# Attention and a gated FFN on one core: fp16 parts of queries and keys, and softmax steps taken in pairs

## The chip, the cores and the metric

The kernel runs on one core of a Trainium2 chip. The metric is the device time of one execution in microseconds, the median of several runs. The core has TensorE (matmuls, PE in the profile), VectorE (DVE), ScalarE (ACT), GpSimd (POOL) and SyncE (SP), which issues all the DMAs here. Each engine works its own instructions in the order in which they were written and waits for the others through semaphores.

## The reference

x has 2 batches of 1024 rows of 512 numbers, all fp32. Weights: Wq, Wk, Wv, Wo of 512 x 512; W1, W3 of 2048 x 512; W2 of 512 x 2048.

```python
xn = layernorm(x)
q, k, v = xn @ Wq.T, xn @ Wk.T, xn @ Wv.T          # 16 heads of 32
scores = q @ k.T / sqrt(32), causal                 # 1024 x 1024 per head
s = softmax(scores) @ v, heads joined, @ Wo.T
h = silu(xn @ W1.T) * (xn @ W3.T)                   # 2048 wide
g = silu(fwht(h) @ W2.T)                            # Walsh-Hadamard, normalised
out = x + s * g
```

## The kernel before, in words

Products that need fp32 accuracy are taken as three products of a high and a low part of each factor (hi x hi, hi x lo, lo x hi). The FFN, V and the probabilities use scaled fp16 parts; Q, K and everything that makes them use float32r parts.

Each of the two batches goes through three stages.

**project(b).** x is normalised (VectorE), transposed in 8 tiles (TensorE, `transpose_xn`, L1418) and split (`xt`, `x16`). TensorE then forms 16 groups of 12 matmuls for Q and K (`group`, L1453; four PSUM banks in turn) and 8 for V. ScalarE copies the high part of each group (L805), VectorE subtracts the low part (L1183), and SP stores both into `qk_parts` in DRAM. In batch 0 ScalarE first splits the weights (L776) as their DMAs land: three tiles of Wq, x, the fourth tile; then after group 1 the four tiles of Wk. VectorE subtracts in the same order, and normalises the second half of x after group 2.

**heads(b).** 16 heads of 12 steps each. `load_stack` brings for each head a stack of 96 rows, Q parts (hi, hi, lo) and K parts (hi, lo, hi), so that one matmul of 96 rows forms the three products. Two more rows hold the negated row maximum (hi and lo) against ones, so that the scores come out of TensorE with their maximum subtracted. The maxima of head n+1 are formed while head n runs: 8 query tiles in the order `MAX_ORDER`, in two matmuls of up to 512 columns for the four longer ones and one for the others (`maxima`, L1554), reduced by VectorE (L1249, or L1251 where it also masks) at the steps `MAX_AT`: 9, 10, 11 of the head before and 0, 1, 3, 4, 5. In batch 0, heads 1 to 15, six of the eight tiles are masked by a further small matmul (L1557) instead. At step 7 TensorE transposes the eight columns of maxima (`transpose_maxima`, L1563), after waiting for the last reduction; ScalarE and VectorE split them (L940, L1257) and two DMAs (L546) write them into the stack's rows for the next head's scores.

A step is a block of 128 keys by up to 512 queries (widths 512, 384, 256, 128, then 512 four times, then 512, 384, 256, 128). Of each step: TensorE forms the scores (`scores`, L1573; two steps are issued together at each even step, each into a bank of its own, and a step of 128 columns is formed 256 wide); ScalarE takes the exponential (`exp`, L868) into one of four buffers `expd`; POOL zeroes the masked triangle of the diagonal steps (`mask`, L699); ScalarE copies to fp16 (`probs_hi`, L878); VectorE subtracts the low part (`probs_lo`, L1264). In ScalarE's order the exponential of step g stands ahead of the copy of step g-1. TensorE multiplies with V in blocks of four steps (`context`, L1591, L1593) at steps 7, 10 and 15, that is step 3 of the next head.

Between these TensorE works off the FFN's 48 matmuls per head (`ffn`, L1613; `FFN_SHARE` says how many at each step). Its results go through ScalarE (`tanh`, L894, one at steps 1 and 7) and VectorE (`gate`, `hide`, L1286 and L1292). The next head's W1 and W3 tiles are scaled (L860) and copied (L931) by ScalarE at steps 1 to 3, and POOL subtracts their low parts in four pieces (`w13_low`, L707). ScalarE copies the output accumulator (`copy_o`, L884) at steps 4 and 8, and POOL joins its halves (`combine`, L713, L718).

In each step the order of an engine's work is written out by hand in its `heads`:

```python
for jm, r in MAX_PLAN.get(g - 1, []):     # VectorE: reductions of the step before
    maxima(n0 + jm, r)
if 1 <= g <= SLOTS:
    probs_lo(n0 * NS + g - 1)
```

**tail(b).** The context is transposed and multiplied with Wo (L1693, L1698); in batch 0 W2 goes through the rest of its Hadamard transform (L1678), its rows loaded by SP once all low parts are done; then the FFN's down projection (L1409 to L1411).

Of the kernel before, what the change touches and what calls it, by code (L numbers as in the profile page):

```python
# [29 lines left out]
P = 128  # L30
# [13 lines left out]
X_TOP = 2048.0  # L44
H_BACK = 2.0 ** -45
# [13 lines left out]
NS = len(STEPS)  # L59
MAX_ORDER = [7, 0, 5, 1, 6, 2, 4, 3]  # L60
NE = 4
# [35 lines left out]
SPLIT_WK_AFTER, ROOT_AFTER = 1, 2  # L97
BUSY_FIRST, BUSY_LAST = 42, 6
# [19 lines left out]

def build(nc, x, wq, wk, wv, wo, w1w3, w2, hadamard, out):

    qk_parts = nc.dram_tensor("qk_parts", [4, D, S], F32R, kind="Internal").ap()
# [4 lines left out]
    with ctx:  # L126
# [27 lines left out]
        g_scale = sb("g_scale", [P, JT], F32)  # L154
        w2_power, w2_scale, h_top, h_top_back, g_back = (
# [15 lines left out]
        with ExitStack() as r:  # L171
            qk_st = [sb(f"qk_st{i}", [P, 2, S], F32R, r) for i in (1, 2)]
# [4 lines left out]
        with ExitStack() as r:  # L177
# [4 lines left out]
            p_hi = [sb(f"p_hi{s}", [P, widths[s]], F16, r) for s in range(NS)]  # L182
            p_lo = [sb(f"p_lo{s}", [P, widths[s]], F16, r) for s in range(NS)]
            squares = sb("squares", [P, 2 * D], F16, r)
            sb("room_after_p", [P, 4 * KT * S - 2 * sum(widths) - 2 * D], F16, r)
# [3 lines left out]
            m_hi = sb("m_hi", [NT, P], F32R, r)  # L189
            m_lo = sb("m_lo", [NT, P], F32R, r)  # L190
            ones_r = sb("ones_r", [P, P], F32R, r)
            qk_lo3 = sb("qk_lo3", [P, W], F32R, r)
# [6 lines left out]
            with ExitStack() as q:  # L199
                qk_hi = [sb(f"qk_hi{i}", [P, W], F32R, q) for i in range(NB)]  # L200
                qk_lo = [*(sb(f"qk_lo{i}", [P, W], F32R, q) for i in range(NB - 1)), qk_lo3]
# [3 lines left out]
            expd = [*stage, sb("expd3", [P, W], F32, r)]  # L205
            scan = sb("scan", [P, 2, D], F32, r)
            sb("room_before_o", [P, 5 * P], F32, r)
            o_sb = [sb(f"o_sb{i}", [P, TPC, VN], F32, r) for i in range(NC)]
            rden = [sb(f"rden{i}", [P, TPC], F32, r) for i in range(NC)]
            qk_st.insert(0, sb("qk_st0", [P, 2, S], F32R, r))  # L210
# [11 lines left out]
        sb("room_after_g_lo1", [P, JT // 2 * D - P], F16)  # L222
# [9 lines left out]
        SB = [bank("s0"), bank("s1")]  # L232
# [16 lines left out]
        proj_ps, proj_hi_done, proj_lo_done = (sem(n) for n in ("proj_ps", "proj_hi_done", "proj_lo_done"))  # L249
        wv_in, wv_abs, bound_ps, v_scale_step, unscale_ps, unscale_done = (  # L250
# [43 lines left out]

        NQ = 2 * KT
# [102 lines left out]

        def diagonal(s):
# [1373 lines left out]
```

## Time and profile before

| | |
|---|---|
| median of 3 runs | 944.87 us (943.33 to 947.14) |
| the profiled execution | 944.66 us, its span 943.0 us |
| TensorE (PE) busy | 928.3 us, 98% |
| VectorE (DVE) busy | 728.0 us, 77% |
| ScalarE (ACT) busy | 625.5 us, 66% |
| GpSimd (POOL) busy | 339.0 us, 36% |
| granted TensorE clock | 0.999 of full speed |
| DMA | 110 MB |
| heads of batch 0 | 88 to 367 us of the span |
| heads of batch 1 | 556 to 829 us |

Matmuls overlap in the profile: the busy time of a matmul is longer than the distance to the next one's start, so that distance is what it costs.

### The profile page before, as it was taken

To read this page: it belongs to the slowest core of one execution; us is meant where nothing else is said; L and a number is where in the kernel's file an instruction comes from. 1 tells how busy PE (TensorE), PEld (TensorE's weight loads), DVE (VectorE), ACT (ScalarE), POOL (GpSimd) and SP (SyncE) were. 2 spreads that over 40 slices of the span, in tenths; PEclk is the share of its full clock that TensorE was granted. 3 is DMA by queue.
4 is the path that set the end of the run, shared out by engine and by line. 5 is a ranking of instruction groups with operands and counts; after the bars stand their busy time and mean duration, and the time that the engine had idled before them with its cause. 6 is when DMAs were issued, how large, how long until landed. Compare 5 with 4: busy or idle time off the path is not lost. (4 is left out here: it accounts for less than half of the span.)

```text
span 943.0 us, 19017 instructions
## 1 busy us (share of the span) xinstructions
PE 928.3 (98%) x6500; PEld 566.6 (60%) x6500; DVE 728.0 (77%) x1416; ACT 625.5 (66%) x1340; POOL 339.0 (36%) x591
## 2 busy tenths in 40 slices
PE   8999999999999999999999999999999999999997
PEld 7764566666666656744468656566665666575443
DVE  7886998998998988846665579989898899833343
ACT  4456889989889877833344358787887888833221
POOL 1896664665665442000000114344344353410000
PEclk9999999999999999999999999999999999999999
DMA  9797245544343414661236622323323232150111
GB/s 291 270 252 228 80 114 151 143 118 118 86 121 90 118 31 124 221 226 44 67 103 244 201 57 80 91 58 95 76 75 92 61 81 58 46 202 22 45 45 45
DMA packets 57920, 110.09 MB, mean 117 GB/s; under 512 B 5600, under 2 KB 22624, under 8 KB 57312
## 3 DMA queue, kind: packets, MB, share of 16 engines
q1 hardware_dynamic: 57824, 108.88, 38.9%
q8 instruction: 52, 0.85, 0.4%
q14 instruction: 44, 0.36, 0.1%
HBM read 79.23 MB, written 29.36 MB: 115 GB/s over the span
## 5 line engine op out<-in xcount | busy, mean ns | idle before, releaser
L1264 DVE TENSOR_TENSOR p_lo<-stages,p_hi 128x512 f16<-128x512 f32 (+2 forms) x288 | 201.7, 710 | 25.3 <-ACT p_hi L878 23.7
L1613 PE MATMUL f<-x_hi,w_lo 128*128 128x512 f16 x512 | 195.6, 382 | 0.0
L1613 PE MATMUL f<-x_lo,w_hi 128*128 128x512 f16 x512 | 194.8, 380 | 0.0
L1613 PE MATMUL f<-x_hi,w_hi 128*128 128x512 f16 x512 | 194.5, 380 | 0.0
L868 ACT ACTIVATE stages<-s 128x512 f32<-128x512 f32 (+2 forms) x288 | 150.6, 524 | 57.9 <-PE s L1573 55.5
L878 ACT ACTIVATE p_hi<-stages 128x512 f16<-128x512 f32 (+2 forms) x288 | 160.5, 557 | 25.6 <-POOL stages L699 16.4
L1573 PE MATMUL s<-qk_st 98*128 98x512 f32 (+2 forms) x384 | 129.9, 416 | 1.7 <-DMA qk_st<-m_lo 1.5
L699 POOL TENSOR_SCALAR_AFFINE_SELECT stages<-stages 128x128 f32<-128x128 f32 x192 | 61.4, 325 | 167.9 <-ACT stages L868 167.4
L707 POOL TENSOR_TENSOR w_lo<-w,w_hi 128x256 f16<-128x256 f32 x128 | 95.5, 775 | 55.2 <-ACT w_hi L931 52.8
L1251 DVE CUSTOM_DVE_ANT_0 m<-m,causal 128x1024 f32<-128x1024 f32 (+1 forms) x98 | 104.5, 1066 | 3.8 <-PE m L1554 2.7
L986 ACT ACTIVATE h_hi<-hidden 128x1024 f16<-128x1024 f32 x32 | 33.8, 1057 | 97.1 <-PE f L1411 97.1
L1332 DVE TENSOR_TENSOR h_lo<-hidden,h_hi 128x1024 f16<-128x1024 f32 x32 | 39.2, 1224 | 76.4 <-ACT h_hi L986 76.4
L1409 PE MATMUL f<-g_hi,h_hi 128*128 128x512 f16 x256 | 97.0, 379 | 0.0
L1410 PE MATMUL f<-g_lo,h_hi 128*128 128x512 f16 x256 | 97.0, 379 | 0.0
L1411 PE MATMUL f<-g_hi,h_lo 128*128 128x512 f16 x256 | 97.0, 379 | 0.0
L1554 PE MATMUL m<-qk_st 96*128 96x512 f32 (+3 forms) x256 | 92.7, 443 | 0.0
L1573 PEld LDWEIGHTS s<-qk_st 98*128 98x128 f32 x384 | 72.4, 191 | 15.3 <-DMA qk_st<-m_lo 3.2
L1613 PEld LDWEIGHTS f<-x_hi,w_lo 128*128 128x128 f16 x512 | 50.0, 98 | 52.1 <-issue 15.2
L1613 PEld LDWEIGHTS f<-x_lo,w_hi 128*128 128x128 f16 x512 | 50.3, 98 | 51.2 <-issue 13.5
L1591 PE MATMUL o<-vparts,p_hi 128*128 128x65 f16 x1152 | 78.0, 191 | 1.0 <-DVE p_lo L1264 1.0
L1591 PEld LDWEIGHTS o<-vparts,p_hi 128*128 128x128 f16 x1152 | 70.4, 96 | 11.0 <-issue 2.8
L1593 PE MATMUL o<-vparts,p_lo 128*128 128x33 f16 x1152 | 76.5, 178 | 0.0
(224 smaller groups left out, 1907.9 us busy)
## 6 DMA issues: line engine op xcount, KB each, us to landing
qk_st<-qk_parts SPq DMA_DIRECT2D x96, 256.0 KB, 4.3
w<-w1w SPq DMA_DIRECT2D x32, 512.0 KB, 3.6
qk_parts<-qk_hi SPq DMA_DIRECT2D x32, 256.0 KB, 3.5
qk_parts<-qk_lo SPq DMA_DIRECT2D x32, 256.0 KB, 4.4
scan<-w1w SPq DMA_DIRECT2D x12, 512.0 KB, 5.6
wht_in<-w SPq DMA_DIRECT2D x4, 1024.0 KB, 10.6
w_butterflied<-wht_in SPq DMA_DIRECT2D x4, 1024.0 KB, 5.7
x_in<-x SPq DMA_DIRECT2D x16, 256.0 KB, 2.9
```

The lines of the kernel that those rows point to most:

```text
L707: pool.tensor_tensor(w13_lo[n % 2][at], w13[at], w13_hi[n % 2][at], ALU.subtract).then_inc(w13_lo_done, 1)
L868: act.activation(expd[q % NE][:, 0:end - need], SB[q % 2][:, 0, need - start:end - start], ACT.Exp).then_inc(exp_done, 1)
L878: act.activation(p_hi[s][:], expd[q % NE][:, 0:end - need], ACT.Copy).then_inc(p_hi_done, 1)
L1251: dve.tensor_tensor_reduce(out=bank, in0=bank, in1=causal[:, S - width:S], scale=1.0, scalar=LOWEST, op0=ALU.add, op1=ALU.max, accum_out=m ...
L1264: dve.tensor_tensor(p_lo[s][:], expd[q % NE][:, 0:end - need], p_hi[s][:], ALU.subtract).then_inc(p_lo_done, 1)
L1409: pe.matmul(o, a_hi, b_hi, start=first, stop=False)
L1410: pe.matmul(o, a_hi, b_lo, start=False, stop=False)
L1411: return pe.matmul(o, a_lo, b_hi, start=False, stop=last)
L1554: mm = pe.matmul(bank[:, at:end], q[0:STACK, t * P:(t + 1) * P], k[0:STACK, at:end], start=True, stop=True)
L1573: pe.matmul(SB[q % 2][:, 0, 0:end - start], k_st[n % NH % 3][0:STACK + 2, k * P:(k + 1) * P], q_st[n % NH % 3][0:STACK + 2, start:end], st ...
L1591: pe.matmul(O[:, 0, first:first + VN], p_hi[s][:, at:at + P], v, start=k == 0 and t == c * TPC, stop=False, skip_group_check=True)
L1613: mm = pe.matmul(F[m][:, 0, :], w, v, start=k == 0, stop=k == GMM - 1)
```

## The change: what it does, and the diff

Queries, keys and the rows of maxima are kept as fp16 parts instead of float32r. So that fp16 holds them, Q and K each get a power of two as a scale, found in batch 0 from the sum of squares of Wq and Wk (eight Squares on ScalarE, two small matmuls, nine small operations of VectorE); the exponential takes the factor back as a per-partition scale. The first score and maxima widths are no longer padded to 256. The two steps (2u, 2u+1) become one pair u: their scores lie side by side, across the border of two PSUM banks, and exponential, mask, copy and subtraction are one instruction per pair. `expd` has two buffers of 1024 columns, no longer in `stages`, and SP no longer waits for the last low part before it loads rows of W2. Cut to its core:

```diff
-NE = 4
+NE = 2
+NP = NS // 2
+SUM_OF_WK_AFTER = 5
-    qk_parts = nc.dram_tensor("qk_parts", [4, D, S], F32R, kind="Internal").ap()
+    qk_parts = nc.dram_tensor("qk_parts", [4, D, S], F16, kind="Internal").ap()
-            m_hi = sb("m_hi", [NT, P], F32R, r)
+            m_hi = sb("m_hi", [NT, 2 * P], F16, r)[:, 0:P]
+            expd = [sb(f"expd{i}", [P, 2 * W], F32, r) for i in range(NE)]
-        SB = [bank("s0"), bank("s1")]
+        S_PAIR = bank("s", 2)
+        SB = [S_PAIR[:, i:i + 1, :] for i in range(2)]
         def score_cols(c, k):
-            return min(need, end - 2 * P), need, end
+            return need, need, end
+        def pair_bank(u):
+            w1, w0 = pair_widths(u)
+            return S_PAIR[:].rearrange("p b w -> p (b w)")[:, W - w1:W + w0]
 # SP
             def load_weight(b, i):
                 if i >= 5:
                     sp.wait_ge(split_lo, split_no(b, i) - 4)
+                    if b == 0:
+                        sp.wait_ge(wqk_sum, i - 4)
-                sp.wait_ge(p_lo_done, (n0 + NH) * NS)
                 if b == 0:
                     sp.wait_ge(wht_stored, D // P * 16)
+                    sp.wait_ge(w13_sum, SCAN_FIRST)
 # POOL
-            def mask(q):
-                pool.wait_ge(exp_done, q + 1)
-                e = expd[q % NE][:, 0:P]
-                pool.affine_select(out=e, in_=e, compare_op=ALU.is_ge, fill=0.0, base=0, pattern=[[1, P]],
+            def mask(n, u):
+                pool.wait_ge(exp_done, n * NP + u + 1)
+                e = expd[(n * NP + u) % NE][:, 0:2 * pair_widths(u)[0]].rearrange("p (a c) -> p a c", a=2)[:, :, 0:P]
+                pool.affine_select(out=e, in_=e, compare_op=ALU.is_ge, fill=0.0, base=0, pattern=[[0, 2], [1, P]],
                                    channel_multiplier=-1).then_inc(mask_done, 1)
-                            pool.wait_ge(exp_done, n * NS + 4 + piece)
+                            pool.wait_ge(exp_done, n * NP + 2 + piece // 2)
                             w13_low(n + 1, piece)
 # ScalarE
+            def wqk_squares(i):
+                act.wait_ge(ssq_ready, 3)
+                if i:
+                    act.wait_ge(wqk_sum, i)
+                act.activation(qk_squares[:], raw[i % 5], ACT.Square, accum_out=qk_ssq[:, i:i + 1]).then_inc(wqk_sum, 1)
             def qk(g):
-                    act.activation(qk_hi[g % NB][:], group_bank(g), ACT.Copy,
-                                   scale=SCALE if QK_GROUPS[g][1] == 0 else 1.0).then_inc(proj_hi_done, 1)
+                    m = QK_GROUPS[g][1]
+                    act.wait_ge(qk_scale_step, qk_scale_steps(m))
+                    act.activation(qk_hi[g % NB][:], group_bank(g), ACT.Copy, scale=qk_scale[:, m:m + 1]
+                                   ).then_inc(proj_hi_done, 1)
                     split_weight(b, KT - 1)
+                    for i in range(KT):
+                        wqk_squares(i)
                     if g == SPLIT_WK_AFTER:
                         for i in range(KT, 2 * KT):
                             split_weight(b, i)
+                            if b == 0:
+                                wqk_squares(i)
             def exp(q):
+                u = q % NP
                 act.wait_ge(scores_ps, q + 1)
                 after(act, p_lo_done, q - NE + 1)
+                act.activation(expd[q % NE][:, 0:sum(pair_widths(u))], pair_bank(u), ACT.Exp,
+                               scale=qk_back[:, 0:1]).then_inc(exp_done, 1)
             def probs_hi(q):
+                if masked_pair(u):
+                    act.wait_ge(mask_done, masks_upto(n, u))
+                act.activation(p_hi[u][:], expd[q % NE][:, 0:sum(pair_widths(u))], ACT.Copy
             def heads(b):
-                    if g < SLOTS:
-                        exp(n0 * NS + g)
-                    if 1 <= g <= SLOTS:
-                        probs_hi(n0 * NS + g - 1)
+                    if g < SLOTS and g % 2 == 0:
+                        exp(n0 * NP + g // 2)
+                    if g < SLOTS and g % 2 == 1:
+                        probs_hi(n0 * NP + g // 2)
 # VectorE
+            def scale_of_qk(m):
+                dve.wait_ge(wqk_sum_ps, m + 1)
+                dve.tensor_reduce(qk_power[:, at], wqk_sum_bank(m), axis=AX.X, op=ALU.add).then_inc(qk_scale_step, 1)
 ...
+                    if b == 0 and g == KT - 1:
+                        scale_of_qk(1)
             def heads(b):
-                    if 1 <= g <= SLOTS:
-                        probs_lo(n0 * NS + g - 1)
+                    if g < SLOTS and g % 2 == 1:
+                        probs_lo(n0 * NP + g // 2)
 # TensorE
                     group(g)
+                    if b == 0 and g == SUM_OF_WK_AFTER:
+                        sum_of_wqk(1)
-                bank, parts = max_parts(t) if t else (X[:, 0, 0:2 * P], [(0, 2 * P)])
+                bank, parts = max_parts(t)
             def scores(q):
-                if s == 0:
+                n, u = divmod(q, NP)
+                if u == 0:
                     pe.wait_ge(m_in, (n + 1) * 32)
-                after(pe, exp_done, q - 1)
+                after(pe, exp_done, q)
+                for s in (2 * u + 1, 2 * u):
+                    c, k = STEPS[s]
+                    start, _, end = score_cols(c, k)
+                    bank = SB[0][:, 0, W - (end - start):W] if s % 2 else SB[1][:, 0, 0:end - start]
+                    mm = pe.matmul(bank, k_st[n % NH % 3][0:STACK + 2, k * P:(k + 1) * P],
+                                   q_st[n % NH % 3][0:STACK + 2, start:end], start=True, stop=True)
+                mm.then_inc(scores_ps, 1)
```

## Rows read from the trace of the kernel before

**Rows 1.** Stretches of the heads; busy us (count) PE, PEld, DVE, ACT, POOL; clock, DMA.
```profile
88.30:366.60 278.30, 277.64 (x2405) 167.56 (x2405) 251.42 (x496) 242.33 (x556) 153.54 (x274) 1.00 0.40 106
545.00:829.00 284.00, 282.50 (x2355) 170.85 (x2353) 252.62 (x562) 228.38 (x530) 119.76 (x250) 1.00 0.27 70
```

**Rows 2.** Timeline, TensorE and VectorE: start us, us, what [idle <- releaser]; two heads.
```profile
238.80 0.68 DVE L1249 TENSOR_REDUCE mx<-xs 128x1 f32<-128x512 f32 x1
239.97 0.27 PE L1563 MATMUL xs<-ident,mx 128*8 128x128 f32 x1
...
676.54 0.57 PE L1573 MATMUL s<-qk_st 98*128 98x512 f32 x2
686.33 0.69 DVE L1251 CUSTOM_DVE_ANT_0 xs<-xs,causal 128x512 f32<-128x512 f32 x1
687.26 0.27 PE L1563 MATMUL xs<-ident,mx 128*8 128x128 f32 x1
...
693.60 0.57 PE L1573 MATMUL s<-qk_st 98*128 98x512 f32 x2
```

**Rows 3.** Timeline of TensorE, part of a head of batch 0.
```profile
241.72 0.38 PE L1613 MATMUL f<-x_hi,w_lo 128*128 128x512 f16 x1
241.94 0.38 PE L1613 MATMUL f<-x_hi,w_hi 128*128 128x512 f16 x1
241.97 0.81 PE L1554 MATMUL m<-qk_st 96*128 96x512 f32 x2
242.63 0.39 PE L1613 MATMUL f<-x_lo,w_hi 128*128 128x512 f16 x1
242.67 0.58 PE L1573 MATMUL s<-qk_st 98*128 98x256 f32 x2
243.09 0.39 PE L1613 MATMUL f<-x_hi,w_lo 128*128 128x512 f16 x1
```

**Rows 4.** Timeline of ScalarE, first part of a head of batch 1.
```profile
676.98 0.60 ACT L868 ACTIVATE stages<-s 128x512 f32<-128x512 f32 x1 [1.50 <-PE s L1573]
...
678.65 0.67 ACT L894 ACTIVATE hidden<-f,w_half 128x512 f32<-128x512 f32 x1
679.22 0.71 ACT L860 ACTIVATE w<-w,w_scale 128x512 f32<-128x512 f32 x1
...
681.64 0.27 ACT L868 ACTIVATE expd<-s 128x128 f32<-128x128 f32 x1
...
682.11 0.62 ACT L931 ACTIVATE w_hi<-w 128x512 f16<-128x512 f32 x1
682.63 0.38 ACT L884 ACTIVATE o_sb<-o 128x260 f32<-128x260 f32 x1
682.90 0.60 ACT L868 ACTIVATE stages<-s 128x512 f32<-128x512 f32 x1
...
684.05 0.65 ACT L878 ACTIVATE p_hi<-stages 128x512 f16<-128x512 f32 x1
```

**Rows 5.** Timeline of POOL in the same head.
```profile
682.08 0.29 POOL L699 TENSOR_SCALAR_AFFINE_SELECT expd<-expd 128x128 f32<-128x128 f32 x1 [1.41 <-ACT expd L868]
...
684.55 3.02 POOL L707 TENSOR_TENSOR w_lo<-w,w_hi 128x256 f16<-128x256 f32 x4
```

**Rows 6.** Timeline of VectorE in the same head, two low parts.
```profile
678.78 0.69 DVE L1264 TENSOR_TENSOR p_lo<-stages,p_hi 128x512 f16<-128x512 f32 x1
...
685.35 1.06 DVE L1264 TENSOR_TENSOR p_lo<-stages,p_hi 128x512 f16<-128x512 f32 x1
```

**Rows 7.** Timeline of ScalarE and TensorE in the first 50 us.
```profile
21.45 0.58 ACT L805 ACTIVATE qk_hi<-xs 128x512 fp32r<-128x512 f32 x1
...
27.12 0.52 PE L1418 MATMUL s<-ident,xb 128*128 128x128 f32 x3 [0.82 <-DVE x_lo L1132]
...
49.38 0.19 ACT L920 ACTIVATION_READ_ACCUMULATOR s<-wht_in 128x1 f32 x1
```

**Rows 8.** Timeline of TensorE at the start of the tail of batch 0.
```profile
370.99 0.47 PE L1678 MATMUL xs<-w_hi,had_r 128*128 128x512 f32 x1 [0.86 <-DVE w_lo L1340]
```

More of the change, by code:

```diff
@@ L411, in load_stack, with masked_pair, masks_upto, pair_widths @@
             for part, of in enumerate((slice(0, 3, 2), slice(0, 4, 3), slice(1, 3))):
[L412 to L413 removed]
+                sp.dma_start(qk_st[n % NH % 3][part * DH:(part + 1) * DH],
+                             qk_parts[of, n % NH * DH:(n % NH + 1) * DH, :].rearrange("w d s -> d w s")
                              ).then_inc(stack_in[n % NH % 3], 16)
[L416 to L418 removed]
+        def masked_pair(u):
+            return diagonal(2 * u) is not None
+        def masks_upto(n, u):
+            return n * (NT // 2) + sum(masked_pair(i) for i in range(u + 1))
+        def pair_widths(u):
+            return widths[2 * u + 1], widths[2 * u]
+        def in_pair(parts, s):
+            w1, w0 = pair_widths(s // 2)
+            return parts[s // 2][:, 0:w1] if s % 2 else parts[s // 2][:, w1:w1 + w0]
+        def pair_bank(u):
+            w1, w0 = pair_widths(u)
+            return S_PAIR[:].rearrange("p b w -> p (b w)")[:, W - w1:W + w0]
         def hidden_part(n, c):
@@ L731, in heads @@
                     n = b * NH + j
-                    for s in range(TPC):
-                        mask(n * NS + s)
+                    for u in range(TPC // 2):
+                        mask(n, u)
                     if j > 0:
@@ L939, in maxima_hi @@
                 after(act, m_in, n * 32)
[L940 removed]
+                act.activation(m_hi[:], X[0:NT, 0, 0:P], ACT.Copy, scale=-1.0 / M_TOP).then_inc(m_hi_done, 1)
             def heads(b):
@@ L1506, in project, with sum_of_wqk @@
                 ffn(b * NH, 0, FFN_PRE)
+            def sum_of_wqk(m):
+                pe.wait_ge(ones_ready, 2)
+                after(pe, proj_lo_done, 4 * m)
+                pe.wait_ge(wqk_sum, (m + 1) * KT)
+                pe.matmul(wqk_sum_bank(m), ones_r[:].bitcast(F32), qk_ssq[:, m * KT:(m + 1) * KT], start=True, stop=True
+                          ).then_inc(wqk_sum_ps, 1)
             def bound_of_v():
@@ L1589, in context @@
                     first = (t - c * TPC) * VN
-                    pe.matmul(O[:, 0, first:first + VN], p_hi[s][:, at:at + P], v, start=k == 0 and t == c * TPC, stop=False,
+                    pe.matmul(O[:, 0, first:first + VN], in_pair(p_hi, s)[:, at:at + P], v, start=k == 0 and t == c * TPC, stop=False,
                               skip_group_check=True)
-                    mm = pe.matmul(O[:, 0, first + DH:first + VN], p_lo[s][:, at:at + P], v[:, DH:VN], start=False,
+                    mm = pe.matmul(O[:, 0, first + DH:first + VN], in_pair(p_lo, s)[:, at:at + P], v[:, DH:VN], start=False,
                                    stop=t == k,
```

136 lines of the change are left out of this document (74 added, 62 removed).

## The prediction

> **What bounds the kernel now.** I read the table by stage first. Over the two head stages, 562 of the 943 us, TensorE is busy 277.6 of 278.3 us and 282.5 of 284.0 us, VectorE 251 and 253 us, ScalarE 242 and 228 us [rows 1]. So TensorE sets the time, with VectorE 10% below it and no engine idle enough to be ignored. Busy TensorE time is no measure of its work, since one matmul's 0.38 us covers the next one's start; I use distances between starts. An fp16 matmul of 512 columns takes 0.22 us from start to start (241.72 to 241.94) [rows 3].
>
> The engines are in-order and tied to each other once per head: at step 7 TensorE transposes the row maxima (L1563) and waits for the eighth reduction of VectorE. In a head of the second batch that reduction (L1251, 686.33, 0.69 us, and about 0.1 us of reading its accumulator) ends at 687.1 and the transposition starts at 687.26; in the first batch the reduction ends at 239.48 and the transposition starts at 239.97 [rows 2]. So this tie has a slack of only about 0.2 us in one batch and 0.4 us in the other, and it decides the case.
>
> **Part 1: fp16 operands on TensorE.** Between the fp16 matmuls at 241.94 and 242.63 lie two fp32r maxima matmuls of 512 columns: 0.69 less 0.22 is 0.47 us, 0.235 each. Between 242.63 and 243.09 lie two score matmuls of 256: 0.24 us, 0.12 each [rows 3]. Fp16 of these widths, scaled from 0.216 for 512, is 0.216 and 0.109, so a matmul gains 0.011 to 0.02 us. A head has 12 score and 12 maxima matmuls: about 0.4 us. Padding to 256 columns also goes: two 128-column score steps and the first maxima tile, 128 columns each, 3 x 0.054 = 0.16 us. Some 0.05 us are small waits. Together 0.62 us a head; 0.35 of it lies ahead of the transposition (8 of the 12 steps), 0.27 behind. For 32 heads that is 19.8 us, if TensorE stays the bound. The scores of a pair wait for the exponential two steps earlier, where now the second waits for that of the step just before: a gain I price at nothing, since those waits are not seen now.
>
> **Part 2: pairs on ScalarE.** One exponential and one copy per pair save starting costs: 0.60 us for 512 columns against 0.27 for 128 is 0.86 ns a column and 0.16 us fixed [rows 4]. Twelve instructions less save ScalarE about 1.5 us a head. Two things are lost. The scale becomes a column of SBUF: the activation that has one and reads PSUM (L894, the row at 678.65) takes 0.67 us where the exponential takes 0.60, so +0.08 each. And now exponential g and copy g-1 alternate, so the mask between them is hidden; a pair's copy follows its own exponential directly. The mask starts 0.17 us after the exponential ends (682.08 against 681.64 and 0.27) and takes 0.29 us [rows 4, 5]. With two blocks of 128 it costs between 0.29 and 0.58; I take 0.43, because one selection of twice the size carries one fixed cost.
>
> **Part 3: one head walked through.** Zero is the start of its first scores (676.54, taken as 676.57, where the matmul ahead ends). Now the first exponential starts at 0.41, the copy of O (L884) at 6.06, the exponential of step 4 at 6.33, and its copy p_hi ends at 684.70, 8.13 [rows 2, 4]. After the change:
> - Two scores instead of one: first exponential at 0.55 (+0.14).
> - Ahead of the O copy stand, besides exponentials and copies, one tanh (0.57 from start to start), two scales (L860, 0.71) and two highs (L931, 0.62), each overlapped by the next instruction for 0.10: 2.83 of the 5.65 us from 676.98 to 682.63. The softmax instructions have the other 2.82. They become: exponential of 896 columns 0.16 + 0.77 + 0.08 = 1.01; mask 0.17 + 0.43 + 0.08 back; copy of 896 columns 0.84; pair 1's exponential 0.45 and copy 0.41, whose mask hides under a high and a scale: 3.39. The O copy moves to 6.78, the exponential of pair 2 to 7.05.
> - That exponential (1024 columns) takes 0.16 + 0.88 + 0.08 = 1.12, its copy 0.65 and 512 more columns, 1.07, with some 0.06 between them and nothing overlapped: the copy ends at 9.31 instead of 8.13.
> - VectorE's order is: sixth and seventh reduction, low part of pair 2, eighth reduction. Now the low part is of step 4 alone (685.35, 1.06 us, then the reduction at 686.33). After: it starts at 9.34 and is 1024 wide, 1.15 us. POOL's w_lo pieces run in the same stretch as now (684.55, four in 3.02 us, 7.98 to 11.0; they hang on the O copy: about 8.1 to 11.1) [rows 5], and of the 1.06 us 0.37 is waiting for such a piece, since p_lo at 678.78 takes 0.69 with POOL idle [rows 6]. A wait between 0 and 0.65 gives an end at 10.5 to 11.15; I take 10.85.
> - Eighth reduction, 0.6 to 0.75 us: ends at 11.55. The transposition can start at about 11.65, while TensorE would be there at 10.69 - 0.35 = 10.34.
>
> That is a stall of 1.3 us in each head of the second batch. In the first, TensorE has mask matmuls ahead of it and the reduction has no accumulator to read, which is why the slack is 0.49 from end to start there and 0.1 to 0.2 here [rows 2]: 0.9 us. Behind it nothing else is late: m_lo and its DMA have more room, as TensorE is later.
>
> What POOL and VectorE do to each other is read as blocking of whole instructions: w_lo pieces of some 0.65 us and p_lo alternate. The Trainium skill, page "SBUF — State Buffer", on its shared port pair, says that whoever starts first holds the pair for the whole instruction and the other blocks. If it were a shared rate (1.06 / 0.69 = 1.54 times) the low part would end at 11.1; by the lock between 10.5 and 11.15. This moves the stall by 0.3 us at most.
>
> 15 heads of each batch have this stall: 15 x 0.9 - 16 x 0.62 = +3.6 us; 15 x 1.3 - 16 x 0.62 = +9.6 us. Heads: +13.
>
> **Part 4: the scales at the start.** ScalarE gets 8 Squares of 512 columns, about 0.8 us each with the accumulator's reading (0.60 as the exponential of that width, and 0.19) [rows 7]. Four, 3.2 us, stand ahead of ScalarE's first copy, beside TensorE's first 24 matmuls, which they outlast by little: no cost, or up to 0.5. The other four lie between the splits of Wk, so ScalarE's third copy (now 21.45) moves by 2.9 us, VectorE's second normalisation with it, and the transposition of x tile 4 (L1418, now 27.12, waiting for VectorE) to about 30.0: +2.9 [rows 7]. Group 5 follows (12 matmuls of 0.23, to 33.1) and the sum (0.3). VectorE waits for it in the second scale (five small dependent steps, some 0.2 each, an estimate), and behind that stands the low part of x (0.6) that the next transposition needs: 35.1 where TensorE is free at 33.4, +1.7. VectorE stays behind until group 8, which needs all eight tiles: I take +1.0. SP's loads of Wk now also wait for the Squares of the tile that they overwrite, which end about with the low parts that they waited for anyway: nothing, up to 0.5; what stands behind them in SP's queue (Wv, a slab of W2) is needed much later. From 28 us to the heads TensorE is full now, so nothing hides this: +5.6, taken as +5.5 us, between +3 (the last two hidden) and +7.
>
> **Part 5: small terms.** The first w2 rows no longer wait for the last p_lo; TensorE's wait of 0.86 us there [rows 8] goes: about -1. Half the bytes of the q and k stacks: nothing, since TensorE barely waits for them; if that cover went it would be under 1 us. POOL's one more memset and the scale column on the q and k copies: under 0.1 us each, beside TensorE's matmuls.
>
> Sum: 943.0 + 13 + 5.5 - 1 = 960.5 of span. The execution itself took 944.66, 1.7 more than its span, and the median shown is 944.87: 962.2 us, which I round to 962.
>
> **Rivals.**
> A. TensorE stays the bound: the maxima are ready in time and part 1 is kept: 944.7 - 19.8 + 5.5 - 1 = 929.4. For it: TensorE fills the stage now, ScalarE loses 1.5 us of work a head, VectorE 0.4. Against: it needs step 7 to come 1.3 us sooner than I walked it. If masks cost 0.29, the scale column nothing and POOL no wait, 0.14 + 0.25 + 0.35 is won, and the stall is still 0.55 us: near A', where 15 x 0.2 + 15 x 0.55 - 19.8 + 4.5 = -4, 941 us.
> B. Slower by more: pairs also make step 11's maxima late. There the first reduction of the next head (1024 wide, 1.2 us) lies behind pair 4's low part, which waits for a masked copy, and TensorE needs it at about the same 17.8 us by my walk. It decides from 0.1 us more on; 0.5 us a head more is +15: 977.
> C. The change doesn't do what it says: fp16 matmuls no faster than fp32r. Against it are the 0.22 us of all fp16 matmuls; then padding alone would gain, and the stall would shrink by as much: within 3 us of my forecast.
>
> **How the numbers follow.** My forecast 0.52 (C in it), own range 950 to 973; A 0.22; A' 0.15; B 0.11. About 0.5%, 4.7 us, is what a measurement can tell from no change: that is 940.1 to 949.6. Half of A' lies below it and half in it, and the forecast's lower edge reaches into it a little: faster 0.29, same 0.10, slower 0.61. The range 929 to 980 leaves out the lower half of A and the upper part of B.
>
> **What would show it.** After the change the transposition L1563's successor should wait for VectorE's reduction of 512 columns, 0.5 to 1.6 us, in nearly every head; heads 17.3 to 18.3 us apart in the second batch (17.06 now, from 676.54 to 693.60 [rows 2]); score matmuls 0.22 us apart; ScalarE idle 0.5 to 0.8 us ahead of the first pair's copy; the tenth group of the projection 5 to 6 us later. I am wrong if heads are 16.4 to 16.6 us apart with TensorE without waits (A), or if waits sit at step 11 (B).

## The result and the profile after

The changed kernel takes 963.01 us (median of 4 runs, 962.87 to 963.33) where the kernel before took 944.10 beside it (median of 4): a ratio of 1.0195, 95% interval 1.0171 to 1.022. It is slower, and by the amount forecast (962). The profiled execution took 963.06 us, its span is 961.3.

Part 1 of the page after:

```profile
PE 919.6 (96%) x6504; PEld 519.3 (54%) x6504; DVE 694.3 (72%) x1233; ACT 627.3 (65%) x972; POOL 322.3 (34%) x464
```

Every engine but ScalarE has fewer busy microseconds than before (TensorE 928.3, VectorE 728.0), and TensorE's share falls from 98% to 96%: the time went into waiting. I cut the span at the first scores of head 0 and head 15 of each batch (distances between starts, so they contain every wait):

| stretch | before | after | difference | forecast |
|---|---|---|---|---|
| start to head 0 | 88.36 | 95.14 | +6.8 | +5.5 |
| 15 heads, batch 0 | 262.42 | 269.08 | +6.7 | +3.6 |
| between | 205.50 | 204.62 | -0.9 | -1 |
| 15 heads, batch 1 | 257.25 | 262.74 | +5.5 | +9.6 |
| rest | 129.42 | 129.76 | +0.3 | 0 |

The forecasts of the two head rows count fp16's gain for 16 heads, as the prediction does, where the rows have 15 distances.

TensorE's waits after, by line and releaser (sum, times, longest):

```profile
PE xs L1653 <- DVE mx L1326: 6.3, 15, 0.4
PE s L1665 <- ACT expd L920: 5.9, 18, 0.9
PE m L1644 <- DVE mx L1326: 5.3, 16, 0.9
PE xs L1653 <- DVE mx L1324: 5.1, 14, 0.4
PE s L1492 <- DVE x_lo L1202: 4.0, 2, 2.4
```

Before, none of these lines was there but the last, with 0.8 us (L1418). L1653 is the transposition of the maxima: 29 waits for VectorE's last reduction. L1665 are scores that wait for an exponential, L1644 maxima that wait for the reduction ahead. The amounts are too small, since a wait is also booked on the weight load or hidden in the modelled end of the matmul ahead; from start to start the transposition loses 0.51 to 0.59 us in each of 29 heads. VectorE's wait for ScalarE's copies, and ScalarE's for POOL's masks:

```profile
DVE p_lo L1338 <- ACT p_hi L929: 97.7, 136, 1.7
...
ACT p_hi L929 <- POOL expd L738: 21.2, 32, 1.0
```

One head of batch 1, timelines of TensorE, ScalarE, POOL and VectorE; zero is 691.75:

```profile
691.75 0.54 PE L1665 MATMUL s<-qk_st 98*128 98x384 f16 x2
...
699.99 0.61 PE L1665 MATMUL s<-qk_st 98*128 98x512 f16 x2 [0.20 <-ACT expd L920]
...
703.09 0.27 PE L1653 MATMUL xs<-ident,mx 128*8 128x128 f32 x1 [0.43 <-DVE mx L1326]
...
708.99 0.50 PE L1644 MATMUL m<-qk_st 96*128 96x384 f16 x2
709.33 0.54 PE L1665 MATMUL s<-qk_st 98*128 98x384 f16 x2
```

```profile
692.33 1.01 ACT L920 ACTIVATE expd<-s,qk_back 128x896 f32<-128x896 f32 x1 [1.31 <-PE s L1665]
693.99 0.95 ACT L929 ACTIVATE p_hi<-expd 128x896 f16<-128x896 f32 x1 [0.65 <-POOL expd L738]
...
698.83 1.11 ACT L920 ACTIVATE expd<-s,qk_back 128x1024 f32<-128x1024 f32 x1
699.97 1.06 ACT L929 ACTIVATE p_hi<-expd 128x1024 f16<-128x1024 f32 x1
...
693.50 0.41 POOL L738 TENSOR_SCALAR_AFFINE_SELECT expd<-expd 128x256 f32<-128x256 f32 x1 [3.08 <-ACT expd L920]
...
699.98 3.54 POOL L746 TENSOR_TENSOR w_lo<-w,w_hi 128x256 f16<-128x256 f32 x4
...
701.06 1.30 DVE L1338 TENSOR_TENSOR p_lo<-expd,p_hi 128x1024 f16<-128x1024 f32 x1 [0.39 <-ACT p_hi L929]
702.28 0.69 DVE L1326 CUSTOM_DVE_ANT_0 xs<-xs,causal 128x512 f32<-128x512 f32 x1
...
707.65 1.23 DVE L1326 CUSTOM_DVE_ANT_0 m<-m,causal 128x1024 f32<-128x1024 f32 x1
```

Read it as my walk: exponential at 0.58 (forecast 0.55); mask 0.41 us (0.43), with ScalarE idle for 0.65 (0.68); pair 2's exponential at 7.08 (7.05), its copy ends at 9.28 (9.31); the low part runs from 9.31 for 1.30 us to 10.61 (10.85) beside POOL's four pieces; the reduction follows, and the transposition starts at 11.34 (11.65). The next head's scores start at 709.33: 17.58 us, against 17.06 [rows 2]. The chain to the transposition is the one forecast.

TensorE loses time in three places of such a head, again from start to start: 0.37 us ahead of step 6's scores (699.99), 0.58 ahead of the transposition (703.09), and 0.20 ahead of step 11's maxima (708.99), which wait for the reduction of 1024 columns at 707.65. Together that is 1.15 us, of which fp16 gives 0.64 back: 0.51 more a head. In batch 0 the three are 0.14, 0.52 and 0.35 us in the usual head, with 0.9 to 1.0 at step 11 in three heads. Batch 1's stretch grew by 5.5 us and not by 15 x 0.51 = 7.7, because before it had some long heads (17.3 to 17.8 us, three of them behind a wait for the rows of maxima), and after it has one (17.86).

The start: TensorE's transpositions of x tiles 4 and 5 with the sum between, ScalarE's third and fifth copies, and VectorE's second scale:

```profile
29.93 0.63 PE L1492 MATMUL s<-ident,xb 128*128 128x128 f32 x4 [2.37 <-DVE x_lo L1202]
...
33.15 0.28 PE L1595 MATMUL f<-qk_ssq,ones_r 128*128 128x4 f32 x2
...
35.03 0.63 PE L1492 MATMUL s<-ident,xb 128*128 128x128 f32 x4 [1.59 <-DVE x_lo L1202]
...
24.23 0.68 ACT L854 ACTIVATE qk_hi<-xs,qk_scale 128x512 f16<-128x512 f32 x1
...
34.39 0.69 ACT L854 ACTIVATE qk_hi<-f,qk_scale 128x512 f16<-128x512 f32 x1 [6.42 <-DVE qk_back L1159]
...
33.47 0.16 DVE L1148 TENSOR_REDUCE qk_power<-f 128x1 f32<-128x4 f32 x1 [3.03 <-PE f L1595]
```

The third copy starts at 24.23 instead of 21.45 and the transposition at 29.93 instead of 27.12 [rows 7], +2.8 each. Then VectorE waits 3.03 us for the sum, with the x low part behind it, so tile 5 waits too; and ScalarE stands 6.42 us in front of a copy whose scale isn't ready. That last number is where room for the Squares is.

### The profile page after: what moved, and what is told of

Its sections match the earlier page's. It is cut to its first block and busy times, and to the rows that moved or that the text cites. A ratio compares the mean times of both kernels' runs of the same rounds, so it can differ in the third digit from the quotient of the medians.

```text
span 961.3 us, 17891 instructions
## 1 busy us (share of the span) xinstructions
PE 919.6 (96%) x6504; PEld 519.3 (54%) x6504; DVE 694.3 (72%) x1233; ACT 627.3 (65%) x972; POOL 322.3 (34%) x464
## 5 line engine op out<-in xcount | busy, mean ns | idle before, releaser
L1338 DVE TENSOR_TENSOR p_lo<-expd,p_hi 128x896 f16<-128x896 f32 (+1 forms) x192 | 194.9, 1015 | 99.7 <-ACT p_hi L929 97.7
L929 ACT ACTIVATE p_hi<-expd 128x896 f16<-128x896 f32 (+1 forms) x192 | 161.6, 842 | 72.8 <-ACT expd L920 31.7
L920 ACT ACTIVATE expd<-s,qk_back 128x896 f32<-128x896 f32 (+1 forms) x192 | 171.2, 891 | 31.5 <-PE s L1665 30.5
L738 POOL TENSOR_SCALAR_AFFINE_SELECT expd<-expd 128x256 f32<-128x256 f32 x128 | 62.9, 491 | 256.0 <-ACT expd L920 256.0
L746 POOL TENSOR_TENSOR w_lo<-w,w_hi 128x256 f16<-128x256 f32 x128 | 109.3, 884 | 56.4 <-ACT w_hi L982 53.9
L1665 PE MATMUL s<-qk_st 98*128 98x512 f16 (+3 forms) x384 | 94.3, 326 | 7.3 <-ACT expd L920 5.9
L1706 PEld LDWEIGHTS f<-x_hi,w_hi 128*128 128x128 f16 x512 | 50.3, 98 | 45.0 <-DVE hidden L1366 1.4
L1644 PE MATMUL m<-qk_st 96*128 96x512 f16 (+3 forms) x256 | 66.4, 340 | 5.8 <-DVE mx L1326 5.3
```

The costliest lines, as they stand in the source:

```text
L746: pool.tensor_tensor(w13_lo[n % 2][at], w13[at], w13_hi[n % 2][at], ALU.subtract).then_inc(w13_lo_done, 1)
L920: act.activation(expd[q % NE][:, 0:sum(pair_widths(u))], pair_bank(u), ACT.Exp, scale=qk_back[:, 0:1]).then_inc(exp_done, 1)
L929: act.activation(p_hi[u][:], expd[q % NE][:, 0:sum(pair_widths(u))], ACT.Copy).then_inc(p_hi_done, 1)
L1338: dve.tensor_tensor(p_lo[u][:], expd[q % NE][:, 0:sum(pair_widths(u))], p_hi[u][:], ALU.subtract).then_inc(p_lo_done, 1)
L1665: mm = pe.matmul(bank, k_st[n % NH % 3][0:STACK + 2, k * P:(k + 1) * P], q_st[n % NH % 3][0:STACK + 2, start:end], start=True, stop=True)
L1706: mm = pe.matmul(F[m][:, 0, :], w, v, start=k == 0, stop=k == GMM - 1)
```

## The experiments

Medians, and the ratio to the kernel before in the same session (943.9 to 944.4 us).

| run | steps | scale | order | median us | ratio (95%) |
|---|---|---|---|---|---|
| 1 | single | column | as before | 951.3 | 1.0079 (1.0058 to 1.0099) |
| 2 | pairs | column | last reduction first | 961.0 | 1.0180 (1.0161 to 1.0198) |
| 3 | pairs | column | both reductions first | 947.9 | 1.0040 (1.0025 to 1.0056) |
| 4 | pairs | column | copies a step later | 1001.5 | 1.0597 (1.0577 to 1.0616) |
| 5 | pairs | column | 3, high part at 5, Squares late | 942.9 | 0.9989 (0.9977 to 1.0001) |
| 6 | single | column | as 5 | 948.0 | 1.0040 (1.0025 to 1.0056) |
| 7 | single | constant | as before | 931.0 | 0.9861 (0.9846 to 0.9875) |
| 8 | pairs | column | 5, high part at 4, early sum | 936.2 | 0.9909 (0.9894 to 0.9924) |
| 9 | pairs | column | 8, maxima's rows ahead of w13 | 936.1 | 0.9909 (0.9897 to 0.9921) |
| 10 | pairs | constant | as changed | 948.3 | 1.0040 (1.0027 to 1.0052) |
| 11 | pairs | constant | as 9 | 927.8 | 0.9829 (0.9817 to 0.9842) |
| 12 | single | constant | as 9 | 942.0 | 0.9984 (0.9971 to 0.9998) |

**Run 1: fp16 parts without pairs.** The change applied to the kernel before, but `exp`, `probs_hi`, `mask`, `probs_lo` and `scores` stay those of single steps.

```diff
+                    act.activation(qk_hi[g % NB][:], group_bank(g), ACT.Copy, scale=qk_scale[:, m:m + 1]
...
-                               ACT.Exp).then_inc(exp_done, 1)
+                               ACT.Exp, scale=qk_back[:, 0:1]).then_inc(exp_done, 1)
```

> This kernel has the fp16 parts, their scales and no padding, but single steps as before: one exponential, copy and subtraction for each. Theory (the pairs' late chain gives the gain of fp16 back, my part 3): TensorE keeps 0.62 us a head, 32 heads 19.8 us, and the start costs the 6.8 us seen in the changed kernel: 944.1 - 19.8 + 6.8 = 931 us, between 926 and 938, with no wait of over 0.2 us at the transposition of the maxima. Rival (fp16 brings TensorE nothing beyond the padding, 0.16 us a head): 944.1 - 5 + 6.8 = 946. Second rival (the scale column's 0.08 us per exponential makes ScalarE late even with single steps): above 950.

951.3: my number, 931, was wrong, and the third reading (the column makes ScalarE late) is the one that fits; run 7, which takes the column out, shows it. Batch 1's heads are 16.97 us apart, so of fp16's 0.62 us only 0.09 is left. TensorE's timeline in such a head shows scores at step 4 as one record of 0.86 us for two matmuls that last 0.54 to 0.60 elsewhere, and the transposition:

```profile
705.15 0.86 PE L1646 MATMUL s<-qk_st 98*128 98x512 f16 x2
...
710.87 0.27 PE L1636 MATMUL xs<-ident,mx 128*8 128x128 f32 x1
```

From start to start the first loses 0.26 us and the transposition 0.29 us. The faster TensorE ran into both of its ties, to ScalarE and to VectorE, at once.

**Runs 2 and 3: the order on VectorE.** In `heads` of VectorE, pair 2's low part (run 2), and pair 4's too (run 3), go behind the reduction of the next slot:

```diff
-                    if g < SLOTS and g % 2 == 1:
+                    if g < SLOTS and g % 2 == 1 and s not in (5, 9):
                         probs_lo(n0 * NP + g // 2)
+                    if g < SLOTS and s - 1 in (5, 9):
+                        probs_lo(n0 * NP + (g - 1) // 2)
```

(run 2 has `(5,)`).

> The changed kernel, but VectorE takes the eighth reduction of a head ahead of the low part of pair 2. Theory (the transposition waits only because that reduction stands behind the late low part): the waits of 0.51 to 0.58 us at 30 transpositions go, 16 us: 963.0 - 16 = 947, between 944 and 952; heads of the second batch 17.0 us apart instead of 17.57. Rival (ScalarE's chain sets the pace of a head and the wait only moves, to the scores of step 6 or the context matmuls): 957 or more.

> As the run before, and the first reduction of the head after (step 11) also ahead of pair 4's low part. Theory: the wait of about 0.36 us at step 11 in the first batch's heads goes too, 15 x 0.36 = 5 us: 942, between 939 and 948. Rival (that wait only appeared because TensorE had been late or is moved by the other wait): within 2 us of the run before.

Run 2 gains 2 us only (961.0, its rival's number), run 3 another 13 (947.9). TensorE's waits in run 2, then in run 3:

```profile
PE m L1646 <- DVE mx L1326: 16.1, 29, 1.3
PE s L1667 <- ACT expd L920: 6.6, 20, 0.9
```

```profile
PE s L1667 <- ACT expd L920: 6.2, 18, 0.9
PE f L1708 <- DVE hidden L1366: 4.0, 10, 0.9
```

In run 2 no transposition waits any more, and most of the wait has moved to the maxima of step 11 (16.1 us, 29 times, in both batches; 5.3 us, 16 times, before this edit). In a usual head of batch 1 the loss there goes from 0.20 to 0.66 us, so 0.46 of the 0.58 won at the transposition is paid back. With both gone, batch 1's heads fall from 17.57 to 16.78 us. What is left in them is 0.37 us ahead of step 6's scores, for ScalarE's exponential of pair 2: 16.78 - 0.37 = 16.41, which is the 17.06 of before less 0.65. So my price for fp16 and the padding, 0.62 us a head, was right. The move of run 3 without that of run 2 wasn't run.

Run 3's second line is a new wait, and a price of the order: in batch 0, with the low part of pair 4 behind the reduction of 1024 columns, VectorE comes late to `hide`. In head 5 of batch 0 it starts 0.03 us before the head in run 2 and 1.16 us after its start in run 3 (the low part of pair 5 ahead of it also takes 1.42 us there instead of 0.65), and TensorE's FFN matmul that needs it loses some 0.5 us in ten of 15 heads. The wait stays in every run with this order: 8 to 11 of 15 heads.

**Run 4: pairs staggered.** ScalarE's copy and VectorE's low part of a pair move one step later, behind the next pair's exponential, to hide the mask.

```diff
-                    if g < SLOTS and g % 2 == 1:
-                        probs_hi(n0 * NP + g // 2)
+                    if g % 2 == 0 and 0 < g <= SLOTS:
+                        probs_hi(n0 * NP + g // 2 - 1)
```

> The changed kernel with both reductions first and, on ScalarE, the copy of a pair one step later, behind the exponential of the next pair, so that the mask between them is hidden as in the kernel before (copy and low part of pair q at the even step where the exponential of pair q+1 is). Theory (the exposed mask is about half of what makes ScalarE late, 0.65 us a head): the waits of the scores at step 6 (0.37 us a head in the second batch) go as well, 15 x 0.37 = 5.5 us: 937, between 931 and 943; floor 931 by the sum of the first run. Rival (the exposed mask was idle time that cost nothing beyond the two reductions' order): within 2 us of the run before.

1001.5 us where 937 was expected, the worst of all, and no answer on the mask. Two waits say why:

```profile
ACT expd L920 <- DVE p_lo L1338: 89.4, 102, 1.9
...
PE xs L1644 <- DVE m_lo L1332: 25.3, 21, 1.6
```

With two buffers `expd` an exponential needs the low part of the pair before last, which now ends later (89 us of ScalarE's idle time, 102 times); and pair 3's low part, which stands ahead of `m_lo` on VectorE in both, now starts 14.37 us into a head of batch 1 instead of 11.40, so that `m_lo` starts at 15.60 instead of 13.46 and the next maxima, which need its bank, wait. I had looked at the engine that I wanted to relieve and not at who waits for what I moved. What the exposed mask alone costs stays open.

**Runs 5, 8 and 9: what is late next.** Run 5 adds to run 3:

```diff
-SCALE_AT, HIGH_AT = [1, 2], [2, 3]
+SCALE_AT, HIGH_AT = [1, 2], [2, 5]
...
                         for i in range(KT, 2 * KT):
                             split_weight(b, i)
-                            if b == 0:
-                                wqk_squares(i)
...
+                    if b == 0 and g == 3:
+                        for i in range(KT, 2 * KT):
+                            wqk_squares(i)
                     for t in XT_AFTER.get(g, ()):
```

> Paired steps with both reductions first (as in the third run), and two moves more: the second high part of w13 goes from slot 3 to slot 5 of a head, behind pair 2's exponential and copy on ScalarE, and the four Squares of Wk go behind the fourth projection copy, where ScalarE waited 6.4 us. Theory: what is left of the waits is ScalarE's late exponential of pair 2 (0.37 us in each head of the second batch, 24 waits of 0.365 in the first), and the high part ahead of it costs it 0.52 us; the start is 2.9 us late through the Squares alone. So batch 1's heads go from 16.78 to 16.41 us, batch 0 loses up to 8.8 us, the start goes from 94.9 to 92.2: 947.9 - 5.5 - 6 - 2.7 = 934, between 929 and 940. Rival (w_lo and the FFN matmuls that need it are late instead, or VectorE is the next bound at once): 943 or more; the start's 2.7 us are to be seen in either case.

942.9, above the expected range and at the rival's number. The usual head of batch 1 is now 16.56 us, the start 92.8 us (a gain of 2.15 of the 2.7), but five heads of batch 1 take 17.1 to 17.9. TensorE's waits:

```profile
PE f L1710 <- DVE hidden L1368: 5.8, 13, 0.9
PE s L1669 <- DMA qk_st<-m_lo: 5.0, 7, 1.2
PE s L1669 <- ACT expd L922: 4.9, 10, 0.9
```

The DMA line has grown (kernel before: 1.5 us in 4 waits; run 3: 1.8 in 2): the scores of the next head wait for its row of maxima, up to 1.2 us. Run 8 moves the high part to slot 4 and the sum from behind group 5 to behind group 4 and its transposition; run 9 swaps two things on SP:

```diff
                         load_stack(sp, n + 2)
-                        load_w13(n + 2)
                     if j + 1 < NH:
                         store_maxima(n + 1)
+                    if j + 2 < NH:
+                        load_w13(n + 2)
```

> As the fifth run (pairs, both reductions first, Squares of Wk late), but the second high part at slot 4 instead of 5, and the sum over Wk's squares after group 4 and its transposition instead of after group 5. Theory: at slot 4 the high part still stands behind pair 2's exponential, so the scores of step 6 don't wait, and POOL's w_lo pieces and what follows are not late, so batch 1's heads are 16.4 to 16.6 us apart throughout (the fifth run: 16.56, but five heads of 17.1 to 17.9 that waited for the rows of maxima); and VectorE waits for the sum 2.7 us less, so TensorE's stalls of 1.8 and 1.7 us in the projection go: start 92.8 to 89.5. Sum: 942.9 - 3.3 - 5 = 935, between 930 and 940. Rival (the irregular heads come from TensorE being faster than the DMA of the rows of maxima, whatever the high part's slot): only the start moves, 940.

> As the eighth run, and on SP's queue the two stores of the rows of maxima go ahead of the load of the w13 tile after next (512 KB, issued 1.9 us ahead of them until now). Theory (the scores waited for those rows because their DMA ran beside that load, 7 waits of up to 1.2 us in the fifth run): these waits go and no head of batch 1 is over 16.7 us: 2 to 5 us less than the eighth run. Rival (the w13 tile then lands too late for its scaling at slot 1, ScalarE waits for it and the gain is lost): equal or slower than the eighth run, with waits of ScalarE's scale for a DMA.

Run 8: start 91.0 (89.5 expected), usual head of batch 1 16.42, 936.2 us. The total is the one expected, but three heads of batch 1 still wait for their row of maxima (17.4 to 17.8 us), as its rival had it. Run 9: two such DMA waits (1.4 us) instead of four (3.8), at the same time within 0.1 us. In its batch 1 no head waits for a row any more, and both of its longest heads (17.18 and 17.65 us) are those in which ScalarE waits for the w13 tile (0.65 and 1.12 us). So the theory and its rival both came true, and they cancel. From run 9, ScalarE's wait, two neighbouring heads' first scores, and TensorE's waits:

```profile
ACT w L916 <- DMA w<-w1w: 1.8, 2, 1.1
```

```profile
655.81 0.54 PE L1670 MATMUL s<-qk_st 98*128 98x384 f16 x2
...
672.27 0.54 PE L1670 MATMUL s<-qk_st 98*128 98x384 f16 x2
```

```profile
PE s L1670 <- ACT expd L923: 5.3, 11, 0.9
PE f L1711 <- DVE hidden L1369: 4.5, 11, 0.9
...
PE s L1670 <- DMA qk_st<-m_lo: 1.4, 2, 1.2
```

16.46 us apart (17.06 before). This is a complete kernel, 0.9% faster than the one before (0.9909, 0.9897 to 0.9921), with all that the change computes. What remains are TensorE's waits for ScalarE and VectorE in batch 0, most of them the one for `hidden` that run 3's order brought, and 2.7 us of the start.

**Runs 6, 7, 10, 11 and 12: the scale column against single steps and pairs.** Run 6 gives single steps run 5's three moves. Run 7 is run 1 with constants, and 10 the changed kernel with constants:

```diff
-                    act.activation(qk_hi[g % NB][:], group_bank(g), ACT.Copy, scale=qk_scale[:, m:m + 1]
+                    act.activation(qk_hi[g % NB][:], group_bank(g), ACT.Copy, scale=1.0
...
-                               ACT.Exp, scale=qk_back[:, 0:1]).then_inc(exp_done, 1)
+                               ACT.Exp, scale=SCALE).then_inc(exp_done, 1)
```

with no `wqk_squares`, `sum_of_wqk` and `scale_of_qk`. Runs 11 and 12 add run 9's order to 10 and 7.

> Single steps with fp16 parts and the same three moves: low parts of steps 4 and 8 behind the reductions of their slot, the second high part at slot 5, the Squares of Wk late. Theory: the two waits per head that the first run showed in batch 1 (0.26 us of the scores for ScalarE, 0.29 of the transposition for VectorE) go: 16.97 to 16.42, batch 0 as much or more: 951.3 - 8 - 8 - 2.7 = 933, between 926 and 940. Rival (single steps with a scale column are 1.0 us a head more on ScalarE than in the kernel before and 1.5 more than pairs, and this sets the pace): 941 or more and slower than the run with pairs.

> The first run's kernel (single steps, fp16 parts) with constant scales: it leaves out the Squares, sums and scale steps, and the exponential and the q and k copies have a constant as scale instead of a column of SBUF (the guard against overflow for large weights is left out). Theory (the column's 0.08 us on each of 12 exponentials is what makes ScalarE late and eats fp16's 0.62 us with single steps, and the start's 6.1 us are the Squares'): start back at 88.4, exponential of 512 columns 0.60 us, batch 1's heads 16.97 to 16.5, batch 0's 17.6 to 17.0: 951.3 - 6.1 - 7 - 9 = 929, between 925 and 934. Rival (the column doesn't matter; VectorE's order in the single-step kernel holds the transposition): 951.3 - 6.1 = 945, heads unchanged.

> The changed kernel (pairs, order as changed) with constant scales, without Squares, sums and scale steps (the guard against overflow for large weights is left out). With the changed kernel, the first and the seventh run it makes a square: single or paired steps, column or constant. Theory: the start is back at 88.4 (-6.8); three of a pair's exponentials lie ahead of pair 2's copy, each 0.08 us shorter, so the wait at the transposition shrinks from 0.55 to 0.3 us and heads by about 0.25 to 0.5: 963.0 - 6.8 - 11 = 945, between 940 and 950; pairs then cost 14 us against single steps at equal scales (seventh run 931). Rival (pairs are not what costs; with the column gone pairs are as good as single steps): 933 or less. Second rival (the column is nothing to pairs): 956.

Run 6 lies at 948.0, 5 us behind run 5 with pairs, so its rival's number held, its reason only in part. Batch 0's stretch is 4.4 us longer than run 5's, with 7.1 us of TensorE's waits for `hidden`; batch 1's is 2.0 shorter, though 0.26 us ahead of step 4's scores stay in each head. Run 7 falls to 931.0, 20 us below run 1, of which the start is 6.1 and the two stretches of 15 heads 5.8 each by the segments of the profiled executions, which are 18.2 us apart. Run 10 is 14.7 below the changed kernel (start 7.0, heads 4.1 and 4.0) and 17.3 above run 7, so with the order as changed pairs cost 17 us against single steps at equal scales. The exponentials by form, of the changed kernel, then of run 10 (busy us, mean ns | idle before):

```profile
L920 ACT ACTIVATE expd<-s,qk_back 128x1024 f32<-128x1024 f32 x26 | 28.7, 1104 | 0.0
L920 ACT ACTIVATE expd<-s,qk_back 128x384 f32<-128x384 f32 x28 | 15.8, 566 | 0.0
```

```profile
L910 ACT ACTIVATE expd<-s 128x1024 f32<-128x1024 f32 x28 | 28.4, 1013 | 0.0
L910 ACT ACTIVATE expd<-s 128x384 f32<-128x384 f32 x28 | 13.3, 474 | 0.0
```

1104 against 1013 ns for 1024 columns, 566 against 474 for 384: the column costs 0.09 us of each instruction, whatever its width. With single steps the same, run 1, then run 7:

```profile
L901 ACT ACTIVATE stages<-s,qk_back 128x512 f32<-128x512 f32 x71 | 49.5, 697 | 16.7 <-PE s L1646 16.7
```

```profile
L891 ACT ACTIVATE stages<-s 128x512 f32<-128x512 f32 x71 | 42.7, 602 | 19.0 <-PE s L1624 18.6
```

So single steps pay it 12 times a head and pairs 6 times. ScalarE's busy time over the 30 heads is 467.0 us in run 1 and 440.3 in run 7, 435.3 in the changed kernel and 419.6 in run 10: the column is 0.9 us a head with single steps, 0.5 with pairs. In run 10 the transposition still waits:

```profile
PE xs L1631 <- DVE mx L1312: 7.3, 14, 0.5
PE xs L1631 <- DVE mx L1310: 4.7, 14, 0.4
```

Its wait did not shrink to 0.3 us, as expected for this run: from start to start it is 0.67 us in batch 1 (0.58 with the column), while the loss ahead of step 6 fell from 0.37 to 0.09 and that at step 11 from 0.20 to 0.10. TensorE is at the transposition sooner, and VectorE is not.

> The ninth run's kernel (pairs, both reductions first, second high part at slot 4, rows of maxima ahead of w13) with constant scales and without Squares, sums and scale steps. Theory (with the order mended pairs have no wait left that the column makes, batch 1 is at its floor of 16.42 us a head already): only the start (91.05 to 88.2) and a little of batch 0 go: 936.1 - 2.9 - 2 = 931, between 928 and 934. Rival (ScalarE is still close behind and the column still counts 0.08 us for every exponential ahead of a wait): 927 or less.

> The seventh run's kernel (single steps, constant scales) with the same order as the ninth: low parts of steps 4 and 8 behind the reductions of their slot, second high part at slot 4, rows of maxima ahead of w13. Theory (TensorE's 0.17 us at the transposition in batch 1 is all that is left, and pairs and single steps have the same floor): batch 1 from 16.58 to 16.42 us a head, 931.0 - 2.4 = 928, between 925 and 931, so pairs bring nothing over single steps where the scale is a constant. Rival (the low parts pushed together make the context matmuls wait, as single steps leave less room): 933 or more.

Run 11: 927.8, a little more than expected: start 88.3, batch 0's stretch 3.6 us shorter than in run 9, batch 1's 2.1, usual head 16.40. Run 12 went wrong, 942.0, for two reasons. The first is the DMA of w13. ScalarE's wait over the whole span, then from the timeline SP's queue and ScalarE's scale in one head:

```profile
ACT w L884 <- DMA w<-w1w: 9.7, 15, 1.7
```

```profile
619.72 0.64 SPq L561 DMA_DIRECT2D qk_st<-m_hi  x1
620.40 0.64 SPq L561 DMA_DIRECT2D qk_st<-m_lo  x1
621.14 1.07 SPq L555 DMA_DIRECT2D w<-w1w  x1
...
627.10 0.72 ACT L884 ACTIVATE w<-w,w_scale 128x512 f32<-128x512 f32 x1 [1.06 <-DMA w<-w1w]
```

The w13 tile is issued at 621.14, behind the rows, and ScalarE stands 1.06 us for it at 627.10. Single steps want that scale 2.65 us after a head's start (pairs at 3.66, both read from regular heads), and here it starts at 3.83. It is run 9's rival, larger here than in run 9. Nine of 15 heads of batch 1 have it (6.3 us), and that stretch is 7.0 us longer than in run 7. The second is the order: in batch 0 TensorE waits 6.1 us, 11 times, for `hidden` (0.3 us in run 7), beside six waits for w13 (3.4 us), and that stretch is 3.3 us longer. How the 3.3 divide isn't shown. Single steps with constants and the mended order, but w13 loaded first, weren't tried; so whether pairs are better than single steps at equal scales and order stays open. Against run 7, which has the old order, run 11 is 3 us better.

## Why the prediction came out, step by step

The total was right to 1 us, and partly by luck: three terms of the sum were off, and they cancelled (batch 0 +3.1 us, batch 1 -4.1, start +1.3).

**Part 1 (0.62 us a head from fp16)** held: 0.65 in run 3 once its wait is taken off, 0.64 to 0.66 in runs 9 and 11 (17.06 against 16.42 and 16.40). A kernel whose ties have 0.2 us of slack can't keep all of it, even without pairs: single steps with a constant scale keep 0.48 and lose 0.18 at the transposition (run 7), with the column they keep 0.09 (run 1).

**Part 2** held in what it loses: mask 0.41, ScalarE's idle time 0.65, column 0.09 instead of 0.08. What it saves was too high: "twelve instructions less save ScalarE about 1.5 us a head", but run 10 against run 7 has 0.7 us a head less of busy ScalarE, since about 0.1 us of each instruction already overlaps the next (682.63 and 0.38 against 682.90 [rows 4]) and only the rest of its fixed 0.16 can be saved; with the column 0.2 us a head is left of it. The walk of part 3 went by single rows and wasn't hurt. What I also let pass was that this column, on 12 single exponentials and with its Squares, is worth 20 us (run 1 against run 7). I had treated it as a detail of pairs.

**Part 3** held as a chain, and the size was off. I had 1.3 us a head in batch 1: 11.65 less 10.34. Measured: 11.34 less 10.76. The low part ended 0.24 sooner than taken, and TensorE came 0.42 later, because it had already lost 0.37 at the scores of step 6. "The scores of a pair wait for the exponential two steps earlier [...]: a gain I price at nothing" was the sentence that failed. Before, step 6's scores waited for step 4's exponential, which ended at 6.33 + 0.60 = 6.93; now they wait for the pair's, which ends at 8.19, where TensorE wants it at about 7.9. At step 11 another 0.20 went, which I had put at nothing ("Behind it nothing else is late"). So batch 1's usual head lost 1.15 where I had 1.3, which is 1.9 of the 4.1 us too much; the other 2.2 are what the long heads of before gave back, which I had not counted. In batch 0 my 0.9 was 0.52, with 0.14 at step 6 and 0.35 at step 11 on top: 1.0 in the usual head, and three heads with 0.6 to 0.7 more.

**Rival B** was therefore half right: step 11 was as close as I wrote ("from 0.1 us more on"). Run 2 shows that it takes most of the transposition's wait over as soon as that is relieved. I gave it a chance of its own where it should have stood behind my forecast as the second wait in line. **Rivals A and A'** needed the maxima in time; run 9 has that, with 2.7 us of the start's cost left where both had 5.5, and is at 936, between the two. A's 929.4 is reached only with constant scales.

**Part 4** forecast each stall in its place: +2.9 (2.81 measured), +1.7 (1.8), +1.0 (1.7 ahead of group 8); the sum lacked 1.3, of which 0.7 is this last one and another 0.7 the wait of head 0's first scores for their row of maxima, 1.27 us from start to start instead of 0.56. **Part 5**, -1: -0.9.

On POOL and VectorE: the low part of 1024 columns took 1.30 us beside the w_lo pieces, and the four pieces 3.54 us against 3.02 [rows 5]. The end at 10.61 lies in the range that blocking of whole instructions gave (10.5 to 11.15) and below the 11.1 of a shared rate. Blocking is what the page "SBUF — State Buffer" of the Trainium skill has; no run took POOL out, so it isn't shown here.

## What to carry to other kernels

Count a saving on the bound engine only up to the slack of its nearest tie to another engine, and look for the tie behind it before pricing the first: here two waits stood one behind the other, and removing the first of them gave 2 us, both 15. Fewer and wider instructions lengthen the path from the first result to the last even where they save busy time; let short work that others wait for (a reduction, a transposition's input) go ahead of the wide one. And when something moves, list who waits for it and what shares its queue: run 4 lost 54 us against run 3 and run 12 lost 11 against run 7 to that.

## What the runs showed of the hardware

A per-partition scale from SBUF costs ScalarE 0.09 us per activation at every width seen, from 128 columns (357 against 263 ns, runs 1 and 7) to 1024 (1104 against 1013). One mask of two 128-column blocks takes 0.41 us against 0.29 for one [rows 5], so some 0.17 us of each is fixed. The DMA of a 2 KB row of maxima was on time in all 15 heads of batch 1's stretch in the changed kernel, where it is issued 3.2 us ahead of the scores that need it (14.4 of 17.6). Issued 2.2 us ahead, it was up to 1.2 us late in three of 15 heads of run 8, with a 512 KB load issued 1.9 us ahead of it, and late in none of run 9 (14.2 into a head of 16.4), where that load stands behind it. It was late in none of run 7 either, with 2.3 us and the load ahead, so these runs don't say what makes it late.
